# Corrections of a position-bias network as sixteen products on 32x32 tiles instead of four on 32x128 tiles

## The reference

```python
pos = grid_q[:, :, None, :] - grid_kv[:, None, :, :]
bias = jnp.sign(pos) * jnp.log1p(jnp.abs(pos))
bias = jax.nn.relu(bias @ cpb_w1 + cpb_b1)
bias = jax.nn.relu(bias @ cpb_w2 + cpb_b2)
bias = (bias @ cpb_w3 + cpb_b3).reshape(b, GROUPS, H * W, Hd * Wd)
sim = jnp.einsum('bhid,bhjd->bhij', qh, kh) + bias
attn = jax.nn.softmax(sim, axis=-1)
```

## Time and profile before

| | |
|---|---|
| Time, median of 3 runs | 898.86 us (898.42 to 899.91) |
| Time of the profiled execution | 897.46 us |
| Its span in the trace | 895.7 us |
| Instructions in the trace | 27530 |
| PE busy (matmuls) | 814.1 us, 91% |
| PE weight loads busy | 232.7 us, 26% |
| DVE busy | 712.5 us, 80% |
| ACT busy | 675.4 us, 75% |
| POOL busy | 66.1 us, 7% |

### The profile page before, as it was taken

How to read it: one execution, slowest core, us unless ns; L and a number is a source line. 1 busy time by engine, 2 the same in 40 slices (tenths; PEclk the granted TensorE clock), 3 DMA queues, 4 the chain that set the end, 5 groups by cost and what they waited for, 6 DMA issues and landing times.

```text
span 895.7 us, 27530 instructions
## 1 busy us (share of the span) xinstructions
PE 814.1 (91%) x12470; PEld 232.7 (26%) x12470; DVE 712.5 (80%) x498; ACT 675.4 (75%) x775; POOL 66.1 (7%) x39
## 2 busy tenths in 40 slices
PE   2399998899999999789999999889999999999997
PEld 1122222232222222223222222222222222222224
DVE  4888798797877588888885868879888668989843
ACT  2468788878776688897876877797878678888863
POOL 3300031300000004030000000311000000000000
PEclk7599999999999999999999999999999999999999
DMA  4502020020110202002020200202002020200000
GB/s 163 120 2 49 2 48 4 12 65 3 43 34 1 48 3 49 12 3 65 2 63 15 49 1 3 49 12 53 15 4 61 14 48 2 72 3 2 2 15 25
DMA packets 18264, 27.67 MB, mean 31 GB/s; under 512 B 10980, under 2 KB 11620, under 8 KB 18148
## 3 DMA queue, kind: packets, MB, share of 16 engines
q1 hardware_dynamic: 18148, 25.91, 11.8%
HBM read 23.05 MB, written 2.74 MB: 29 GB/s over the span
## 4 chain that ended last, share of the span: by engine, by line
issue 59%; PE 26%; POOL 6%; ACT 5%; DVE 3%; DMA 0%; SPq 0%; ACTq 0%; POOLq 0%
PE pair L892 9%; PE scores L910 8%; POOL conv_prod L357 4%; ACT h L489 3%; POOL big L470 2%; PE pair L866 2%; DVE h L643 2%; PE pair L1045 1%; PE scores L921 1%; PE pair L1000 1%; PE pair L1018 1%; PE pair L1036 1%; PE scores L1006 1%; ACT big L591 0%; DMA const<-consts_dram 0%
## 5 line engine op out<-in xcount | busy, mean ns | idle before, releaser
L643 DVE TENSOR_TENSOR h<-hxy 128x2048 f32<-128x2048 f32 x256 | 578.4, 2288 | 76.5 <-PE pair L892 72.4
L489 ACT ACTIVATE h<-pair 128x1024 f32<-128x1024 f32 x512 | 517.2, 1023 | 143.5 <-PE pair L866 108.1
L892 PE MATMUL pair<-h,wts 32*32 32x512 f32 x8192 | 300.1, 603 | 17.0 <-ACT h L489 5.5
L910 PE MATMUL scores<-h,wts 128*32 128x512 f32 x2048 | 277.5, 610 | 0.1
L866 PE MATMUL pair<-fy,u_rows 32*128 32x512 bf16 x1024 | 103.1, 389 | 14.5 <-DMA fy<-fy_dram 14.5
L866 PEld LDWEIGHTS pair<-fy,u_rows 32*128 32x128 bf16 x1024 | 26.4, 91 | 233.6 <-issue 233.6
L892 PEld LDWEIGHTS pair<-h,wts 32*32 32x32 f32 x8192 | 66.1, 103 | 78.9 <-ACT h L489 34.5
L910 PEld LDWEIGHTS scores<-h,wts 128*32 128x32 f32 x2048 | 42.4, 108 | 157.5 <-issue 148.8
L357 POOL TENSOR_TENSOR conv_prod<-qpad,wts 128x288 f32<-128x288 f32 x16 | 34.0, 2150 | 426.5 <-ACT qpad L516 426.5
L1000 PE MATMUL pair<-const,probs 128*128 128x128 f32 x128 | 21.2, 291 | 21.5 <-ACT h L489 20.8
L499 ACT ACTIVATE probs<-scores,wts 128x512 f32<-128x512 f32 x32 | 22.0, 688 | 23.8 <-PE scores L910 23.5
(11 more groups left out here) (101 smaller groups left out, 376.0 us busy)
## 6 DMA issues: line engine op xcount, KB each, us to landing
hxy<-features_dram SPq DMA_DIRECT2D x64, 256.0 KB, 4.9
wts<-weights_dram SPq DMA_DIRECT2D x2, 960.0 KB, 8.1
att_den<-reciprocals_dram SPq DMA_DIRECT2D x7, 256.0 KB
x<-x_dram SPq DMA_DIRECT2D x2, 512.0 KB, 5.5
fy<-fy_dram SPq DMA_DIRECT2D x16, 64.0 KB
fy_dram<-fy_part SPq DMA_DIRECT2D x24, 32.0 KB, 3.8
out_dram<-x SPq DMA_DIRECT2D x3, 256.0 KB, 5.4
features_dram<-pos_sign SPq DMA_DIRECT2D x4, 128.0 KB, 2.3
```

The costliest lines, as they stand in the source:

```text
L489: emptied("z", 2 * g + j, act.activation(h2[j][g % H2_BUFS][:].rearrange("p r n -> p (r n)"), pair_of("z", 2 * g + j)[:], ACT.Relu))
L643: dve.tensor_tensor(h1[g % H1_BUFS][:].rearrange("p c (y x) -> p c y x", x=W), hx[unit % 2][:, :, t].unsqueeze(2).broadcast_to([128, CT, H ...
L892: ins = pe.matmul(z_of(g, r)[32 * c:32 * (c + 1)], w(l, "w2")[key_rows(r), key_rows(r)], h1[g % H1_BUFS][key_rows(r), c], start=r >= 2, st ...
L910: ins = pe.matmul(scores[phase % 2][32 * r:32 * (r + 1)], w(l, "w3")[:, 32 * t:32 * (t + 1)], h2[rows[0] // 2][step % H2_BUFS][:, r % 2], ...
```

## The change

Each correction is cut by columns: per key row four matmuls of 32 x 32 weights, each with its own quarter of the partitions of the bank, in place of one of 32 x 128. The corrections of rows 0 and 1 of the step now stand ahead of those of rows 2 and 3 of the step before. The wait for the pair of rows 2 and 3 moves from ahead of layer 2 to ahead of its third row. The waits for `fy` and `u` are asked once per segment instead of once per unit of 16 steps.

```diff
--- before.py
+++ after.py
@@ -863,31 +863,34 @@
 
                 unit, h, t = g // UNIT_STEPS, g // STRIDES % 2, g % STRIDES
                 y = fy[unit // PAIRS % 2][key_rows(r), t, unit % PAIRS, H // 2 * h:H // 2 * (h + 1)]
-                return pe.matmul(z_of(g, r), u_rows[unit // PAIRS // B][key_rows(r)],
-                                 y.unsqueeze(2).broadcast_to([32, H // 2, W]), **flags)
+                for c in range(CT):
+                    ins = pe.matmul(z_of(g, r)[key_rows(c)], u_rows[unit // PAIRS // B][key_rows(r), key_rows(c)],
+                                    y.unsqueeze(2).broadcast_to([32, H // 2, W]), **flags)
+                return ins
 
             def corrections(g):
 
 
-                if g:
-                    correction(g - 1, 2, start=False, stop=True)
-                    filled("z", 2 * (g - 1) + 1, correction(g - 1, 3, start=False, stop=True))
                 if g < ALL_STEPS:
                     unit = g // UNIT_STEPS
-                    if g % UNIT_STEPS == 0:
+                    if unit % PAIRS == 0 and g % UNIT_STEPS == 0:
                         pe.wait_ge(fy_loaded, 16 * ROWS * (unit // PAIRS + 1))
                         pe.wait_ge(u_ready, unit // PAIRS // B + 1)
                     turn("z", 2 * g)
                     correction(g, 0, start=True, stop=False)
                     correction(g, 1, start=True, stop=False)
+                if g:
+                    correction(g - 1, 2, start=False, stop=True)
+                    filled("z", 2 * (g - 1) + 1, correction(g - 1, 3, start=False, stop=True))
 
             def layer2(g):
 
 
                 l = g // UNIT_STEPS // PAIRS // B
-                turn("z", 2 * g + 1)
                 pe.wait_ge(h1_ready, g + 1)
                 for r in range(ROWS):
+                    if r == 2:
+                        turn("z", 2 * g + 1)
                     for c in range(CT):
                         ins = pe.matmul(z_of(g, r)[32 * c:32 * (c + 1)], w(l, "w2")[key_rows(r), key_rows(r)],
                                         h1[g % H1_BUFS][key_rows(r), c], start=r >= 2, stop=r < 2)
```

## The result

The changed kernel takes 907.83 us (median of 4 runs, 907.22 to 910.89) against 898.64 us before on the same chip: a ratio of 1.011, 95% interval 1.0096 to 1.0124. It is about 1.1% slower, where I had forecast 1% faster. The profiled span goes from 895.7 to 905.4 us, by 9.7.

A forecast was written before the change was run, and what follows sets the result against it. PE's own work was taken to set the pace, ACT following closely. Savings of 9.7 + 5.6 - 3.4 - 2.5 = 9.4, say 9 us, took the profiled 897.46 to 888.5, forecast median 890.0 us, range 876 to 898.

The forecast's parts named there:

- More instructions: On PE, 12 more loads and matmuls per step: sixteen corrections start within 0.05 to 0.08 us and cost nothing.
- The last sign of being wrong: In layer 2: the forecast is wrong if L892's own stretch grows by what L866's lost.
- the overhead per matmul: On PE: some 60 cycles per matmul, starts 0.025 us apart, sixteen taking 0.4 us; about 970 us, chance 0.02.
- Tiles: Between corrections and layer 2: one change of shape goes, saving 0.10 us per step (0.085 to 0.115).
- rival 3: Between corrections and layer 2: the 0.115 us stays and twelve more starts add 0.04 to 0.08; 908 to 917, chance 0.11.
- Order within the corrections: The correction releasing ACT's second relu comes 14 places later, at 3.3 ns each: 0.05 us later, upper end 0.09.
- ACT's run to the transpose: ACT's gapless 4.30 us from L866 to L1000: its start moves by +0.05; 31 phases lose 3.4 us in all.
- Just-in-time steps: Steps where layer 2 just gets its relu: PE stands still 0.04 us, keeps 0.06 of 0.10; 93 steps, 5.6 us.
- the steps with room: 97 PE-bound steps where layer 2 waits for no relu: 0.10 us saved each, 9.7 us.
- The moved wait: Second pair's wait, now before layer 2's rows 2 and 3: 0.05 us off steps that hang on it.
- The waits for other stages: 35 steps waiting for other stages gain nothing and take back about 0.07 us each, -2.5 us.

The follow-up runs named there:

- e1: The kernel before with the sixteen corrections on 32x32 tiles alone, order and waits as before: 911.28 us, ratio 1.0142.
- e3: The changed kernel with the corrections of row 2 left out, twelve per step: 897.96 us, one run.
- e4: The changed kernel without the corrections of row 2 and three of the four of row 3, nine per step: 897.85 us, one run.
- e6: The changed kernel with each of the sixteen corrections cut into two of 256 columns: 927.54 us, one run.
- e8: The kernel before with only the corrections of rows 0 and 1 put first, tiles and waits as before: 897.04 us, ratio 0.9982.
- e5: The kernel before with only the wait for the second pair moved ahead of row 2 of layer 2: 897.70 us, ratio 0.9983.

## Why the prediction was wrong, point by point

**The step that failed** is "More instructions": sixteen corrections "cost PE nothing". The last sign of being wrong that I had named is what came, and more: L892's own stretch grew by 0.17 us where the junction lost 0.10. I weighed only the pace, the time between two starts and the mean over a dense stretch (L981, 0.027 us per product). The pace was fine: sixteen corrections started within the forecast 0.05 us. What binds is how many can be under way at once. The row of L981 could not show that: its products have 128 columns and last 0.27 us each, so that some ten are under way at once. The old trace gave cause to ask, though not the limit: layer 2 is sixteen products of four instructions, 64, and they came in when the corrections were through or nearly so. That 64 fit shows there, that no more do only in e1, e3, e4 and e6. So this term cost 0.17 us per plain step, not 0.

**A rule passed over.** The Trainium skill, TensorE: Matmul & The Clock Gate (table at the head, Engine queue depths), gives PE a queue of 64 entries with a partial reorder window that pulls weight loads ahead of running matmuls. The counts agree with it: in the changed kernel, e3, e4 and e6 the 65th instruction is the last to get in, behind one load that is through. That an entry is kept until the matmul is through is read from the same runs (0.41 us with 512 columns, 0.30 with 256); that loads count beside matmuls isn't shown, as said at e4. The rule that I did weigh, the overhead per matmul, rightly had a small chance: sixteen corrections span 0.43 us from first start to modelled end, not 0.4 in starts alone.

**Tiles.** Right: 0.226 us for L867 to L895, in the forecast 0.21 to 0.24. On one shape of tiles the groups hand over tile by tile, across bf16 and fp32 too. So rival 3 (the junction still empties the array) is refuted, although its 908 to 917 begins right where the time came out (907.83): right sign, other mechanism.

**Order within the corrections.** Mis-sized. ACT's relu starts 0.55 us after L867 (68.09 to 68.64), 0.12 later than before and not 0.05, beyond my upper end of 0.09 too. The runs show why: I counted 14 places at 3.3 ns, the distance of two starts, but the relu moves by 8.3 ns for each matmul that stands ahead in the group. It starts 0.430 us after the first correction when the second matmul releases it (before), 0.446 at the fourth (e8), 0.480 at the eighth (e1), 0.513 at the twelfth (e3) and 0.547 at the sixteenth. The relus of e1 and e3 behind the corrections at 825.25 and 822.29:

```profile
825.73 1.03 ACT L489 ACTIVATE h<-pair 128x1024 f32<-128x1024 f32 x1 [0.57 <-PE pair L867]
```

```profile
822.80 1.02 ACT L489 ACTIVATE h<-pair 128x1024 f32<-128x1024 f32 x1 [1.38 <-PE pair L867]
```

ACT's run to the transpose, 4.30 us before, is now 4.37 (68.09 to 72.46), for a forecast of +0.05. The same order also gained something I hadn't seen, the 0.02 us of e8.

**Just-in-time steps.** Not reached. PE's step grew instead of shrinking, so the relus had more room, not less: PE's waits for a relu ahead of the transpose went from 20.8 us to 18.9. The sum of 5.6 us for them, and the 9.7 us for the steps with room, have no counterpart.

**The moved wait.** I gave it 0.05 us in just-in-time steps and nothing in those that wait for other stages. e5 shows the reverse: a plain step keeps its length, and some 1.5 us come from the others.

**The waits for other stages** take back, as forecast, but this time they took back part of a loss: 16 us of longer steps became 9.7.

## What to carry to other kernels

Before cutting a matmul into more and smaller ones, count what must be under way at the same time, loads and matmuls, from the first one that isn't through to the last one that should run beside it; a pace that looks easy says nothing about that. Here 64 fit (or, which no run tells apart, 32 matmuls with their loads), and an fp32 product takes four of them. When a junction between two shapes of tiles goes, ask what it had kept apart: before, the corrections were almost through when layer 2 came in, so its 64 instructions had the room to themselves.

## What was not expected of the hardware

- By the counts, a matmul holds its place for its whole way through the array: a correction's tile is free again after 0.21 us (layer 2 starts at 0.226), but the places of the first corrections serve new products only at about 0.41.
- Cutting corrections in halves at equal work costs 20 us (927.54, one run, against 907.83).
- Putting the corrections of rows 0 and 1 first shortens layer 2 by 0.02 to 0.03 us even on the old tiles (e8). What makes its sixteenth product late in the old order wasn't settled.
- A later place in a group delays the signal by more than the start: a matmul starts 3.3 ns after the one before it, but the relu it releases moves by 8.3 ns per place (0.430 us at the second, 0.547 at the sixteenth). So the signal of the sixteenth correction reaches ACT 0.07 us later than its start explains. No run shows what takes the other 5 ns.
- Matmuls on free tiles overtake others: in e3 two products, in e4 four, start some 0.1 us ahead of the eight that stand before them in the program (read from the counts; the timeline doesn't name single tiles).
